# A gated cross-attention and mixture kernel on one core: the first tile's score maxima are split around the first attention units, and the second tile's statistics go behind the keys by heads

## The reference

```python
x = x + tanh(g_xattn[0]) * L0_xattn(ctx, layernorm(x), Wq, Wk, Wv, lambdas)   # 32 half heads of 8
x = x + tanh(g_ffn[0])   * L0_ffn(layernorm(x), W1, b1, W2, b2, Wa, Wb)       # 3 of 8 zones by a router
x = x + tanh(g_xattn[1]) * L1_xattn(layernorm(x), ctx, ctx, Wq, bq, Wo, bo)   # 16 heads of 16
x = x + tanh(g_ffn[1])   * L1_ffn(layernorm(x), w_gate, w_up, w_down)
```

```python
att = softmax(einsum('bhtd,bhnd->bhtn', q, k) * scale)        # h = 32 half heads, n = 77
att = att[:, even] - lam * att[:, odd]
out = einsum('bhtn,bhnd->bhtd', att, v)
```

## Time and profile before

| | us |
|---|---|
| median of 3 runs (lowest, highest) | 678.16 (677.62, 679.12) |
| the profiled execution, its own time | 677.06 |
| its span, first to last instruction | 675.2 |
| PE busy | 610.4 (90% of the span) |
| DVE busy | 386.4 (57%) |
| ACT busy | 361.8 (54%) |
| POOL busy | 148.4 (22%) |
| mean granted clock of TensorE | 0.985 of full speed |

### The profile page before, as it was taken

The page is one execution under the profiler, slowest core; times in us unless marked ns, Lnnn a source line. Parts: engine busy times, 40 slices in busy tenths (PEclk is TensorE's granted clock), DMA queues, the critical chain, the costliest instruction groups (busy, mean ns, idle before and its releaser), DMA issues.

```text
span 675.2 us, 11620 instructions
## 1 busy us (share of the span) xinstructions
PE 610.4 (90%) x4336; PEld 500.8 (74%) x4336; DVE 386.4 (57%) x841; ACT 361.8 (54%) x615; POOL 148.4 (22%) x218
## 2 busy tenths in 40 slices
PE   2688888888699999999999999999888998999998
PEld 2564555544389899999989888989666786878887
DVE  6668667779573523425545534534586564656654
ACT  4335758566875745646557535535685424443421
POOL 9615265254640000000000000000474300210000
PEclk9779999999999999999999999999989899999999
DMA  7302120122031030120303250020041100000000
GB/s 230 101 15 85 25 57 21 48 50 98 5 115 39 1 125 1 36 90 1 126 7 90 60 161 1 1 96 2 15 127 51 47 1 2 33 2 11 22 32 32
DMA packets 22551, 34.76 MB, mean 51 GB/s; under 512 B 4704, under 2 KB 13280, under 8 KB 22496
## 3 DMA queue, kind: packets, MB, share of 16 engines
q1 hardware_dynamic: 20224, 30.51, 14.7%
q0 software_dynamic: 1984, 3.44, 2.1%
q10 hardware_dynamic: 288, 0.07, 0.1%
HBM read 18.93 MB, written 2.10 MB: 31 GB/s over the span
## 4 chain that ended last, share of the span: by engine, by line
PE 72%; DVE 12%; ACT 5%; issue 4%; POOL 3%; DMA 1%; ACTq 0%; DVEq 0%; POOLq 0%
PE PV L1256 22%; PE SC L1284 20%; PE SC L1256 9%; PE PV L1275 4%; DVE NM L1131 4%; PE AUX L1256 3%; PE AUX L1366 3%; PE PV L1284 2%; PE SC L1404 2%; PE AUX L1284 2%; DVE O L1139 2%; ACT XN L848 1%; ACT PB L903 1%; PE AUX L1323 1%; DVE ST L1050 1%
## 5 line engine op out<-in xcount | busy, mean ns | idle before, releaser
L989 DVE TENSOR_TENSOR HL<-HF,HH 128x512 fp32r<-128x512 f32 x96 | 67.1, 699 | 154.6 <-ACT HH L945 154.5
L903 ACT ACTIVATE PB<-SC 77x1024 f32<-77x1024 f32 x96 | 95.4, 1014 | 59.2 <-PE SC L1404 59.0
L1284 PE MATMUL SC<-WBH,HL 128*128 128x256 f32 x384 | 108.7, 283 | 0.0
L1284 PE MATMUL SC<-WBL,HH 128*128 128x256 f32 x384 | 108.6, 283 | 0.0
L1284 PE MATMUL SC<-WBH,HH 128*128 128x256 f32 x384 | 108.6, 283 | 0.0
L945 ACT ACTIVATE HH<-PV 128x512 fp32r<-128x512 f32 x96 | 57.3, 597 | 71.8 <-PE SC L1284 71.8
L940 ACT ACTIVATE HF<-PV 128x512 f32<-128x512 f32 x96 | 57.5, 599 | 54.7 <-PE PV L1256 52.6
L713 POOL TENSOR_TENSOR RSTD<-RSTD,NHALF 128x4 f32<-128x4 f32 x16 | 17.9, 1116 | 291.5 <-DVE RSTD L1063 291.4
L1256 PE MATMUL PV<-XH,WAH 128*128 128x512 f32 x192 | 77.6, 404 | 1.0 <-DVE O L1139 1.0
L1284 PEld LDWEIGHTS SC<-WBL,HH 128*128 128x128 f32 x384 | 72.7, 189 | 3.9
L1284 PEld LDWEIGHTS SC<-WBH,HH 128*128 128x128 f32 x384 | 72.5, 189 | 4.0 <-DVE HL L989 0.3
(11 more groups left out here) (259 smaller groups left out, 1224.5 us busy)
## 6 DMA issues: line engine op xcount, KB each, us to landing
QG<-QH SPq DMA_DIRECT2D x96, 64.0 KB, 2.0
WSA<-in_wa SPq DMA_DIRECT2D x6, 1024.0 KB, 5.0
WSB<-in_wb SPq DMA_DIRECT2D x12, 512.0 KB, 6.7
QG<-QL SPq DMA_DIRECT2D x48, 64.0 KB, 2.0
X<-in_x SPq DMA_DIRECT2D x4, 512.0 KB, 6.0
QG<-QH POOLq DMA_DIRECT2D x32, 64.0 KB, 2.3
out_x<-X SPq DMA_DIRECT2D x8, 256.0 KB, 2.2
QG<-QL POOLq DMA_DIRECT2D x16, 64.0 KB, 2.2
```

The costliest lines, as they stand in the source:

```text
L903: act.activation(probs(n)[0:S, :, :], scores(n)[0:S, :, :], ACT.Exp, scale=SCALE[a]).then_inc(exp_done, 1)
L989: return dve.tensor_tensor(dst, raw, hi.bitcast(F32), ALU.subtract)
L1284: ins = pe.matmul(ps[:, D * (t % 2):D * (t % 2 + 1)], lhs[:, block], rhs, start=first and t == 2 * i and n == 0, stop=last and t == 2 * i ...
```

## The change

Three things are done to the list. (1) The second tile's statistics, `norm(ATT0, 1)`, move from ahead of the key pieces 1 and 2 to behind the keys by heads. (2) Of the eight `max` steps of `second`, four stay ahead of unit 0, and the other four are spread over units 0 and 1; `negpart` 1, which needs all eight, moves behind unit 1. (3) The 16 `max` steps of tile 0's second half are spread over units 2 to 4 and no longer over 0 to 4. Tiles 1 to 3 and all that follows keep their lists.

```diff
-    steps += keys(0, 0, 1) + [("query", 0, 0)] + moves(0, 0) + norm(ATT0, 1) + keys(0, 1, 3) + [("heads", 0, 0)]
+    steps += keys(0, 0, 1) + [("query", 0, 0)] + moves(0, 0) + keys(0, 1, 3) + [("heads", 0, 0)] + norm(ATT0, 1)
     first, second = ([("max", 0, 0, t, 2 * i + u) for t in range(TT) for u in range(2)] for i in range(2))
-    steps += [("scale", ATT0, 1)] + first + [("negpart", 0), ("turn", ATT0, 1)] + second + [("negpart", 1)]
+    steps += [("scale", ATT0, 1)] + first + [("negpart", 0), ("turn", ATT0, 1)] + second[:4]
     left = []
     for j in range(J):
         side = {}
         last = (5, 5, 5, 4)[j]
-        fillers = [(maxima(0, j, 1), 0, last)]
+        fillers = [(maxima(0, j, 1), 0 if j else 2, last)]
+        if j == 0:
+            fillers.append((second[4:], 0, 2))
+            side.setdefault(1, []).append(("negpart", 1))
```

## The result

| | before | after |
|---|---|---|
| median of the runs (lowest to highest), us | 678.25 (676.87 to 679.94, 20 runs) | 679.53 (678.66 to 681.73, 20 runs) |
| ratio of after to before | | 1.0019, 95% interval 1.0010 to 1.0028 |
| profiled execution, us | 677.06 (span 675.2) | 681.73 (span 679.9) |
| mean granted clock of the profiled execution | 0.985 | 0.977 |

The change makes the kernel slower by 1.3 us, about 0.2%, and the interval of the ratio does not contain 1. The profiled execution of after is the slowest of its twenty, and that of before is one of its faster ones, so the two traces lie further apart (4.7 us) than the medians (1.3), and they are read beside the experiments' traces.

A forecast was written before the change was run, and what follows sets the result against it. PE's chain was taken as the bound, carrying the opening's waits for DVE on to the end. A gain of 0.7 against 1.17 for three reductions gave +0.45; from the runs' median 678.16, forecast 678.5, range 676.7 to 680.2.

The forecast's parts named there:

- unit 8 between 60 and 62 us: Sign for the forecast: unit 8 expected at 60.7; a start before 60 or after 62 would prove it wrong.
- Part 1: Opening on DVE: statistics behind the keys by heads start the first reduction at 27.6 instead of 27.37; cost +0.25 us.
- Rival 4: POOL's moves for the first scores are held off by DVE's selections: first reduction at 28.5, total 679.4; chance 0.02.
- Part 2: Four reductions fewer ahead of the first attention scores: unit 0 at 35.9, 3.1 earlier, and unit 1 3.6 earlier.
- Part 3: Late maxima in units 0 and 1: DVE waits for ACT before the coefficients, query at 45.2, last QL 0.8 earlier.
- Part 4: Behind the query, ahead of unit 8: three more reductions on DVE cost 1.17, giving -0.7 + 1.17 = +0.45.
- rival 2: DVE's gaps of 0.68 and 0.85 behind the query hide the three added reductions: 677.5; chance 0.11.
- The sum: Whole kernel: +0.45 on the profiled 677.06 gives 677.5; from the runs' median 678.16, forecast 678.5, no change.
- Rivals 1 and 3: 1: full clock through V's projections, 676.8 or 678.0, chance 0.26; 3: half clock on the query, 681.2, chance 0.10.
- rival 1: Full clock through V's projections, 676.8 (0.16), or partly, 678.0 (0.10); cites a rule that transposes don't count as busy.

The follow-up runs named there:

- e2: The changed kernel with the second tile's statistics back in their old place, so only the maxima are moved; median 679.44 us, ratio 1.0013 to before.
- e1: The kernel before with only the second tile's statistics moved behind the keys by heads; median 678.95 us, ratio 1.0013 to before.
- e6: The changed kernel with 34 unused matmuls in PE's waits throughout the opening, to keep the clock full; median 676.86 us.
- e5: The kernel before with 32 unused matmuls in PE's waits throughout the opening, to keep the clock full; median 676.14 us.
- e9: e6 with the first tile's maxima of the second key part woven in from unit 1 instead of unit 2; median 676.53 us.
- e3: The changed kernel with nine unused matmuls in PE's two waits ahead of the query; median 677.69 us, ratio 0.9997 to before.
- e7: The changed kernel with the coefficients moved from unit 1 to unit 2, just ahead of the query's residues; median 678.58 us, ratio 0.9997 to before.
- e8: e7 with e6's unused matmuls except the six ahead of the fourth late score; median 676.72 us.
- e12: The changed kernel with the coefficients late as in e7, maxima from unit 1 as in e9, and the unused matmuls; median 673.68 us, ratio 0.9939 to before.
- e11: e5 run again unchanged, the kernel before with unused matmuls, for more executions; median 676.27 us.
- e4: The kernel before run again unchanged, for a second trace and more mean clocks; median 677.35 us, ratio 1.0001.

## Why the prediction was right, and where it was off

The forecast was no change, 678.5, and 679.53 lies in the range; but the measured ratio's centre is at the edge of what I called no change, and its sign is plain. That the number came out so near is in part luck. The forecast named its own test, unit 8 between 60 and 62 us, and no trace of the changed kernel or of its parts passed it cleanly: in after unit 8 starts at 63.16, with the 1.05 off 62.1, and in e2 at 59.82. The errors have opposite signs: the clock was full where I had half, and half where I had full. By the steps:

- **Part 1** (+0.25; first reduction at 27.6). Counted without the 1.05 that was there before, it came 0.37 later in after (28.79), and e1 ends at +0.14. Right within its bounds. Rival 4 did not come: POOL issues the moves in 0.50 each, though the selections took 2.06 and not 1.92. By the port lock of the Trainium skill (SBUF — State Buffer, "Who interferes with whom") selections in a two-port mode that get the ports first would have held up the issues. Whether they run in such a mode no run shows; in this trace no issue is stretched, in that of before one of the eight took 0.80:

```profile
L745 POOL DMA_DIRECT2D QG<-QH x8: 496/498/502, 21.6 to 26.9; - x8
```

- **Part 2** (unit 0 at 35.9, unit 1 3.6 earlier). At 36.91 and 39.30, with the 1.05 off 35.86 and 38.25: right for unit 0. Unit 1 came 5.1 earlier than its 43.36 in the trace of before, not 3.6, because V's projections, which I priced at half clock, ran at full.
- **Part 3** (DVE waits 1.4, coefficients end 44.3, query at 45.2, last QL 0.8 earlier). The wait was 1.45, and A fell by 0.84, but in the profiled run two errors cancel there: with the 1.05 off, the query began at 43.57 and not 45.2, since the units before it ran at full clock, and then lost most of that at half clock. **This is the step that failed**: it took the 0.8 as a gain of the order that the clock leaves alone. At a full clock (e6 against e5) the last QL comes 0.03 earlier; with the one half-clock stretch of e2 it comes 2.65 earlier. The 0.8 was worked out with V's projections at half clock in both kernels.
- **Part 4** (three reductions, +1.17). Right: B is 10.56 to 10.62 in all six traces with the old order and 11.72 to 11.78 in the four with the new one that have neither a fall nor e9's edit. I took the path's end and not the hidden one, and rival 2 falls: the gaps that were to swallow them are still there in e6, 0.68 and 0.84.
- **The sum.** +0.45 was part 4 less part 3's gain. Part 4 stands at 1.14; it is part 3's gain that failed, since without the clock's help nothing stands against it. The full-clock pair's traces give +1.1, and the medians of before and after +1.3; that the two agree does not make them the same thing, as below. The sum also took it that a microsecond in the opening is a microsecond of the span. The time from unit 8 to the end was not the same in all traces, 614.8 to 618.4 us, and in e2 and e3 the falls near 138 and behind used up what the opening had won.
- **Rivals 1 and 3** both happened in the profiled execution: full clock from 35.5 through V's projections, and half clock on the query from 45.7, at 0.43 a matmul as priced. I gave them 0.26 and 0.10 as alternatives, but one execution had both. The mean clock over the runs is 0.981 both before and after, so the change moves half-clock stretches rather than adding to them. That the rows speak against what rival 1 cites on transposes was read too strongly: nine scores stood beside the twelve transposes, so the rows decide nothing. From the traces with and without them, half-clock stretches cost A 3.5 in before (28.55 against e5's 25.07). In the new order the long first one costs 0.9 (e2 against e6), the fall at the query 1.8 more (27.71 against 25.90) and the one at the values 1.5 (B). How often each happens the runs don't tell, since they give only a mean clock each.

What is shown, then, is that at a full clock the new order delays unit 8 by 1.1, and through which reductions. That the runs' 1.3 is this same loss is argued, not shown. For it speak that after is slower at the same mean clock too, and that e7, which moves only the coefficients, takes the loss back without a higher mean clock. Against it stand e2 and e3: at the ordinary clock their openings are 1.3 to 1.4 shorter than before's, and the time is lost again at falls of the clock behind unit 8. How often each case comes one trace per kernel can't tell. Part 4's reductions and part 3's wait are two separate losses on one path: e9 takes back 0.8 at unit 8, the late coefficients 1.44 (A, e8 against e6), and e12 both, 36.76 - 34.56 = 2.20.

## What to carry to other kernels

When maxima, reductions or other small work of one engine are shifted from ahead of a first consumer to behind it, count what then stands between the next two big steps on that engine: at a full clock the early consumer gained 2.4 us here and none of it reached unit 8, but three reductions more did. A wait for a third engine inside an in-order list (the coefficients behind ACT's exponential) belongs where its engine is idle anyway; moved there, it gave back about what the change had cost. And before a gap-ridden opening is tuned by order, compare the orders at the same clock, as with unused matmuls in the gaps, and look at the runs too: up to unit 8 one trace of nearly this order read as 1.4 us faster than before and another as 1.9 us slower, while the runs of both were slower by 1.1 to 1.5 in the mean.

## What was not expected of the hardware

- Unused matmuls in waits of PE pay for themselves: 1.8 us off the old order and 2.6 off the new one (means of 676.44 for e5 with e11, and 677.09 for e6).
- The first rise of the granted clock came at 16.3 to 18.5 us (before, after, e1 to e4 and e7) in code that none of them changes there, and the first tile's last QL ended at 21.14 to 22.20, mostly the later the later the rise. Over the 101 runs of before the time falls as the mean clock rises (correlation -0.75; 677.4 us at 0.985, 679.3 at 0.977), so more than half of this kernel's scatter goes with the clock.
- A fall of 3.4 us has no one price: 1.8 on the query, 1.5 on the values behind it, 0.8 and 1.2 at 141 and 189.
- Nearly the same order (part 1 apart) with the same wait of PE ahead of the query kept the full clock in one execution (e2) and lost it in another (after).
